# Gates as three bf16 parts in both expert mixtures, weight loads in pieces, and two projection jobs moved, in a 12-stage perceiver kernel

## The reference, cut to what matters

```python
# L1_ffn: one expert of eight, its gate is a sigmoid
logits = x @ gate_w.T; sel = argmax(logits); rw = sigmoid(max(logits))
for e in range(8):
    xs = x * (rw * (sel == e))[:, None]
    out = out + (xs @ w_up[e].T) * silu(xs @ w_gate[e].T) @ w_down[e].T
# L2_ffn: two experts of eight, gates a softmax over both, and two shared experts without a gate
logits = x @ router_w + router_b
gates = softmax(logits where it is among the two largest, else -inf)
out = sum_e gates[:, e] * expert_e(x) + shared_0(x) + shared_1(x)     # expert = silu(x w1) * (x w3) @ w2
# L3_xattn: keys and values of all 8192 context rows
k = context @ k_w.T + k_b;  v = context @ v_w.T + v_b;  16 heads of 16 channels, masked softmax
```

## Time and profile before

| | |
|---|---|
| time, median of three runs | 1553.99 us (1551.33 to 1559.85) |
| profiled execution, its own time | 1555.07 us |
| its span in the profile | 1553.2 us |
| PE busy | 1501.2 us, 97% of the span |
| DVE, ACT, POOL busy | 838.6, 639.3, 151.7 us |
| mean granted clock of PE | 0.994 |

### The profile page before, as it was taken

One profiled execution on the slowest core, in us unless ns is written; L12 is line 12 of the kernel. 1 busy time (PEld: TensorE's weight loads), 2 busy tenths in 40 slices (PEclk: granted clock), 3 DMA queues, 4 the chain that ended last, 5 costly groups with the idle time before them and its releaser, 6 DMA issues.

```text
span 1553.2 us, 24376 instructions
## 1 busy us (share of the span) xinstructions
PE 1501.2 (97%) x9939; PEld 960.1 (62%) x9950; DVE 838.6 (54%) x1488; ACT 639.3 (41%) x1213; POOL 151.7 (10%) x191
## 2 busy tenths in 40 slices
PE   8999999999999999999999999999999999998898
PEld 3667656886668655567655544555555554645697
DVE  5652645643432533432362258889899983566422
ACT  1212342122432423433353246777777775404121
POOL 0000340002000212200102051100000000100000
PEclk9999999999999999999999999999999999999999
DMA  9134132221023420112215166464567404100140
GB/s 373 58 108 175 69 119 89 82 82 62 0 83 114 154 69 28 38 58 104 81 42 177 65 157 123 80 93 69 122 140 180 67 4 182 65 34 1 48 170 14
DMA packets 40406, 146.87 MB, mean 95 GB/s; under 512 B 6092, under 2 KB 21708, under 8 KB 30668
## 3 DMA queue, kind: packets, MB, share of 16 engines
q1 hardware_dynamic: 40296, 145.32, 32.5%
HBM read 122.73 MB, written 22.56 MB: 94 GB/s over the span
## 4 chain that ended last, share of the span: by engine, by line
PE 87%; DVE 8%; ACT 3%; issue 1%; DMA 0%; SPq 0%; ACTq 0%; DVEq 0%
PE PS L162 54%; PE PS L2107 8%; PE PS L2019 7%; PE PS L2004 5%; PE PS L612 3%; PE PS L1434 2%; DVE SM L2123 1%; PE PS L1628 1%; PE PS L1446 1%; PE PS L2636 1%; PE PS L1641 1%; DVE CN L2687 1%; PE PS L2098 1%; PE PS L1648 1%; PE PS L2569 1%
## 5 line engine op out<-in xcount | busy, mean ns | idle before, releaser
L2123 DVE TENSOR_REDUCE SM<-PS 128x1 f32<-128x1024 f32 x256 | 301.7, 1219 | 35.4 <-PE PS L2004 34.2
L162 PE MATMUL PS<-CT,HT 128*128 128x512 f32 x416 | 190.4, 593 | 0.7 <-ACT HT L719 0.7
L162 PE MATMUL PS<-CN,AR 128*128 128x256 f32 (+1 forms) x832 | 188.0, 371 | 0.0
L162 PEld LDWEIGHTS PS<-CN,AR 128*128 128x128 f32 x832 | 151.0, 190 | 44.0 <-issue 28.7
L2019 PE MATMUL PS<-AR 49*128 49x256 bf16 (+1 forms) x1216 | 163.5, 272 | 3.0 <-issue 2.4
L162 PE MATMUL PS<-HT,AR 128*128 128x512 f32 x328 | 149.5, 605 | 2.6 <-ACT HT L346 1.6
L2019 PE MATMUL PS<-AR,CT 49*128 49x256 bf16 (+1 forms) x832 | 125.2, 272 | 0.0
L669 DVE TENSOR_REDUCE SM<-AR 128x1 f32<-128x512 f32 x96 | 65.7, 686 | 97.2 <-ACT AR L725 95.6
L162 PEld LDWEIGHTS PS<-CT,HT 128*128 128x128 f32 x416 | 73.6, 190 | 68.4 <-issue 66.0
L162 PEld LDWEIGHTS PS<-HT,AR 128*128 128x128 f32 x328 | 60.7, 191 | 86.1 <-issue 82.0
L162 PE MATMUL PS<-AR 128*128 128x256 f32 (+3 forms) x504 | 109.8, 372 | 1.4 <-DVE AR L647 0.8
(11 more groups left out here) (340 smaller groups left out, 2142.5 us busy)
## 6 DMA issues: line engine op xcount, KB each, us to landing
CN<-ctx_n SPq DMA_DIRECT2D x24, 1024.0 KB, 4.7
AR<-k_parts SPq DMA_DIRECT2D x114, 128.0 KB
CT<-pack SPq DMA_DIRECT2D x7, 2048.0 KB, 8.4
k_parts<-CN SPq DMA_DIRECT2D x32, 384.0 KB, 3.3
AR<-pack SPq DMA_DIRECT2D x20, 512.0 KB, 4.8
CT<-k_parts SPq DMA_DIRECT2D x78, 128.0 KB
CN<-v_ones SPq DMA_DIRECT2D x8, 1152.0 KB, 10.3
v_ones<-CN SPq DMA_DIRECT2D x29, 288.0 KB, 2.9
```

Of the source, the lines that this page charges most:

```text
L162: last = te.matmul(o, l, r, start=first and k == 0, stop=final and k == n - 1, skip_group_check=True)
L2123: ve.tensor_reduce(MX9[:, p % 2, e, g % 8 // 4, g % 4:g % 4 + 1], PS[:, b:b + 2, :].rearrange("p a b -> p (a b)"), AX, ALU.max).then_inc(* ...
```

## The change

It does these things, in the diff's order:

1. `esel` becomes bf16 (half the bytes), with ones for every row r whose r mod 8 is e, 48 rows in all; a bf16 identity `idb` is loaded too.
2. The gates are split into three bf16 parts whose sum is the fp32 gate. R has 24 columns in stage 5 and 48 in stage 8 (three parts for each of two choices). The four transposes and the per-expert product are bf16: one matmul with K = 24 or 48, in place of one fp32 matmul with K = 8.
3. The routing chains on DVE change: in stage 5 four small instructions for the parts, threaded through the chain, and a wider last product. In stage 8 the second choice's push is one instruction, only the second logit's exponential is taken, the weights are 1/(1+ex) and ex/(1+ex), four instructions split them, and two products make R.
4. `up` is cut in `gate` and `up`. Stage 5: `gate(0)`, the transposes, half job 0, `up(0)`. Stage 8: `gate(0)`, `up(0)`, the `r8` job, the transposes, `gate(1)`.
5. Stage 8's half jobs `h8` go. That value job is dealt to `s9` in place of a key job, and this key job to `heads`, at g = 33.
6. Stage 10's weights come in eight transfers of up to 512 KB at g = 81, 83, ... 95, each behind the scores of the step before. The fetches that stood at the first step of pair 8 (g = 64) stand at g = 67, behind a score of that pair.

```diff
-    "s5": [("gate", 16), ("esel", 1024)] + ...
+    "s5": [("gate", 16), ("esel", 512), ("idb", 64)] + ...
-                             ("s7", "v"), ("b8", "kvkv"), ("t8", "k"), ("r8", "v"), ("h8", "v"), ("b9", "vvk"),
-                             ("t9", "k"), ("s9", "kvvkvvvkvv"), ("heads", "k" * 4)):
+                             ("s7", "v"), ("b8", "kvkv"), ("t8", "k"), ("r8", "v"), ("b9", "vvk"),
+                             ("t9", "k"), ("s9", "kvvkvvvvvv"), ("heads", "k" * 5)):
...
+        def gate_rows_pe(pe, s, R, idb):
+            b, before = PB.take(("rt", s), ("rt", s))
+            pe.wait_ge(*before, ("R", s))
+            for i in range(4):
+                z = pe.e.transpose(PS[:, b, 0:256].bitcast(BF16)[0:R.shape[2], tok(i)], R[:, i, :], idb)
+            z.then_inc(*pe.inc("turned", "rt_ps", s))
...
-                up(0)
-                jobs_pe(pe, f"r{s}")
-                rows8_pe(pe, s, R)
-                half_pe(pe, f"h{s}", 0)
+                gate(0)
+                if gate_first:
+                    gate_rows_pe(pe, s, R, idb)
+                    half_pe(pe, f"h{s}", 0)
+                    up(0)
+                else:
+                    up(0)
+                    jobs_pe(pe, f"r{s}")
+                    gate_rows_pe(pe, s, R, idb)
+                    gate(1)
                 for e in range(n):
...
-                        te.matmul(PS[:, b, :], W["esel"][0:8, e * 128:e * 128 + 128], RT, start=True, stop=True,
+                        te.matmul(PS[:, b, :], esel[0:RT.shape[0], e * 128:e * 128 + 128], RT, start=True, stop=True,
...
                     if e + 1 < n:
+                        if e or gate_first:
+                            gate(e + 1)
                         up(e + 1)
                     if e:
                         down(e - 1)
-                half_pe(pe, f"h{s}", 1)
+                if gate_first:
+                    half_pe(pe, f"h{s}", 1)
                 down(n - 1)
...
+            ve.tensor_copy(parts5[:, :, 0], rw5).then_inc(*dv.inc("route", "rw_p0", 5))
...
+            ve.tensor_tensor(rest5, rw5, parts5[:, :, 0], ALU.subtract).then_inc(*dv.inc("route", "rw_rest", 5))
+            ve.tensor_tensor(parts5[:, :, 1], rw5, parts5[:, :, 0], ALU.subtract).then_inc(*dv.inc("route", "rw_p1", 5))
...
+            ve.tensor_tensor(parts5[:, :, 2], rest5, parts5[:, :, 1], ALU.subtract).then_inc(
+                *dv.inc("route", "rw_p2", 5))
+            dv.wait_ge(("oh", 5), ("rw_p2", 5))
+            ve.tensor_tensor(R5.rearrange("p a (k e) -> p a k e", k=3),
+                             oh5.unsqueeze(2).to_broadcast([128, 4, 3, 8]),
+                             parts5.unsqueeze(3).to_broadcast([128, 4, 3, 8]), ALU.mult).then_inc(
+                *dv.inc("route", "R", 5))
...
-        for p in range(4):
+        for p in range(5):
             PAIR_JOBS[8 * p + 1] = jobs.pop(0)
...
+        W10_PIECES = [(to[:, c:min(c + 1024, to.shape[1])], src[:, c:min(c + 1024, to.shape[1])])
+                      for to, src in (w10_load, w10_more) for c in range(0, to.shape[1], 1024)]
+        W10_AT = {81 + 2 * i: piece for i, piece in enumerate(W10_PIECES)}
...
-                if what in ("beside", "both") and n % 8 == k == 0:
+                if what in ("beside", "both") and n % 8 == (3 if n // 8 == 8 else 0) and k == 0:
...
+                    if p == 8:
+                        used.append(("st_ps", 9, 8, 4, 1))
...
-                if what == "beside" and (n, k) == (80, 0):
-                    sp.wait_ge(("job_ps", "k", 31), ("job_ps", "v", 31))
-                    for load in (w10_load, w10_more):
-                        se.dma_start(*load).then_inc(*sp.lands("w10", "w", 10))
+                if what == "beside" and k == 0 and n in W10_AT:
+                    sp.wait_ge(("job_ps", "k", 31), ("job_ps", "v", 31), ("st_ps", 9, n // 8, 2 * (n % 8) - 1, 1))
+                    se.dma_start(*W10_AT[n]).then_inc(*sp.lands("w10", "w", 10))
```

More of the change, by code:

```diff
@@ L32 @@
     "s4": [("Wq", 512), ("Wk", 512), ("Wv", 512), ("gamma", 1)],
-    "s5": [("gate", 16), ("esel", 1024)] + [(f"{k}{e}", 256) for e in range(8) for k in ("g", "u", "d")],
+    "s5": [("gate", 16), ("esel", 512), ("idb", 64)] + [(f"{k}{e}", 256) for e in range(8) for k in ("g", "u", "d")],
     "s6": [("Wq", 512), ("Wk", 512), ("Wv", 512), ("bq", 2), ("bk", 2), ("bv", 256)],
@@ L36 @@
            ("dsel", 128), ("rows", 4)],
-    "s8": [("rw", 16), ("rb", 32), ("esel", 1024)] + [(f"{k}{e}", 256) for e in range(10) for k in ("g", "u", "d")],
+    "s8": [("rw", 16), ("rb", 32), ("esel", 512), ("idb", 64)] + [(f"{k}{e}", 256) for e in range(10) for k in ("g", "u", "d")],
     "s9": [("Wq", 512), ("Wk", 512), ("Wv", 512), ("bq", 2), ("bk", 2), ("bv", 256), ("sum34", 34),
@@ L1414, in experts, with gate @@
             ready = lambda e: ("h", s, "gated" if gate_first else "row" if e < n_gated else "up", e)
+            esel, idb = W["esel"].bitcast(BF16), W["idb"].bitcast(BF16)
             def pe_part(pe):
                 te = pe.e
-                def up(e):
-                    wg, wu = mat(W[f"g{e}"], 2), mat(W[f"u{e}"], 2)
+                def gate(e):
+                    wg = mat(W[f"g{e}"], 2)
                     b, before = PB.take(("g", s, e), ("g", s, e))
@@ L1849, in dve_8 @@
             dv.wait_ge(("oh", 8))
-            ve.tensor_scalar(l8, oh8, -3e38, None, ALU.mult).then_inc(*dv.inc("route", "out", 8))
-            dv.wait_ge(("out", 8))
-            ve.tensor_tensor(l8, l8, lg8, ALU.add).then_inc(*dv.inc("route", "lg2", 8))
-            first_of_max_dve(dv, 8, "oh2", l8, top8b, eq8b, m8b, oh8b, ("lg2", 8))
-            dv.wait_ge(("oh2", 8))
-            ve.tensor_tensor(oh8b, oh8b, oh8, ALU.add).then_inc(*dv.inc("route", "both", 8))
-            ve.tensor_tensor(ex8, lg8, up8(top8), ALU.subtract).then_inc(*dv.inc("route", "under", 8))
@@ L1857, in dve_8 @@
[L1857 to L1864 removed]
+            ve.scalar_tensor_tensor(out=l8, in0=oh8, scalar=-3e38, in1=lg8, op0=ALU.mult, op1=ALU.add).then_inc(
+                *dv.inc("route", "lg2", 8))
@@ new lines, in dve_8 @@
+            dv.wait_ge(("lg2", 8))
+            ve.tensor_reduce(top8b, l8, AX, ALU.max).then_inc(*dv.inc("route", "oh2_top", 8))
+            dv.wait_ge(("oh2_top", 8))
+            ve.tensor_tensor(ex8, top8b, top8, ALU.subtract).then_inc(*dv.inc("route", "under", 8))
+            ve.tensor_tensor(eq8b, l8, up8(top8b), ALU.is_equal).then_inc(*dv.inc("route", "oh2_eq", 8))
+            dv.wait_ge(("oh2_eq", 8))
+            ve.tensor_tensor(eq8b, eq8b, CS["iota8"].rearrange("p (a b) -> p a b", b=8), ALU.mult).then_inc(
+                *dv.inc("route", "oh2_w", 8))
@@ new lines, in dve_8 @@
+            dv.wait_ge(("w_rest", 8), ("w_p1", 8))
+            ve.tensor_tensor(parts8[:, :, 2, :], rest8, parts8[:, :, 1, :], ALU.subtract).then_inc(
+                *dv.inc("route", "w_p2", 8))
+            dv.wait_ge(("w_p2", 8), ("oh2", 8))
+            for n, oh in enumerate((oh8, oh8b)):
+                ve.tensor_tensor(R8[:, :, 24 * n:24 * n + 24].rearrange("p a (k e) -> p a k e", k=3),
+                                 oh.unsqueeze(2).to_broadcast([128, 4, 3, 8]),
+                                 parts8[:, n].rearrange("p k a -> p a k").unsqueeze(3).to_broadcast([128, 4, 3, 8]),
+                                 ALU.mult).then_inc(*dv.inc("route", "R", 8))
@@ L3026, in _constants @@
     c["ones2"] = (np.arange(128)[:, None] % 64 == 32).astype(np.float32)
-    esel = np.zeros((128, 8, 128), np.float32)
-    for e in range(8):
-        esel[e, e, :] = 1.0
-    c["esel"] = esel.reshape(128, 1024)
+    esel = np.zeros((128, 8, 128), np.uint16)
+    for r in range(48):
+        esel[r, r % 8, :] = 0x3F80
+    c["esel"] = esel.reshape(128, 1024).view(np.float32)
+    c["idb"] = (np.eye(128) * 0x3F80).astype(np.uint16).view(np.float32)
     inv = (1.0 / np.float32(10000.0) ** (np.arange(0, 64, 2, dtype=np.float32) / np.float32(64))).astype(np.float32)
```

68 lines of the change are left out of this document (50 added, 18 removed).

## The result

The changed kernel takes 1543.75 us (median of 19 executions, 1538.3 to 1551.3) where the kernel before took 1553.99 us on the same chip (19 executions, 1549.0 to 1559.9). The ratio is 0.9934, its 95% interval 0.9919 to 0.9948: 10.2 us faster. The forecast was 1544.3 us, the range 1538.5 to 1551.5. The total is right. Three terms of the sum are not (the slot of a gate's product, the start of stage 5, and stage 9 beside its large transfers), and a part of the agreement is luck.

The account below looks back on a forecast made before the run. The prediction took PE to bound the kernel, busy 1501.2 of 1553.2 us. Stage 5 -4.8, stage 8 -6.65 and the key job +1.83 gave -9.6, so 1544.3 us from the median 1553.99; range 1538.5 to 1551.5.

Parts of the forecast that it names:

- The slot of a gated expert: Stages 5 and 8, PE time for the gate's product: 0.53 us in place of 1.16, 0.63 less in each of sixteen.
- The 0.1 that was to come back at a bank: Stage 5: 0.1 us regained because expert 1's second product no longer waits for a bank.
- K and the passes: The gate's bf16 product: K = 24 is not slower by its rows than K = 8; K = 49 streams at 0.213 us.
- The start of stage 5: Longer DVE chain to R delays the transposes and the first gate's product: 0.35 us lost, bounds 0 to 1.2.
- Stage 8: Eight slots -5.0, half jobs gone -0.95 and -0.9, +0.2 back: -6.65 us, with R 2 us ahead.
- The key job: Stage 9, key job added at g = 33: +1.83 us, eight steps taking 23.66 us in place of 21.83.
- The transfers: Stage 10's weights in eight transfers in place of two: 0, since the window around the two took 21.84 us.
- The prediction's own sign of being wrong: PE gaps named "issue" at the weight pieces, or PE waiting for RT or a bank in the mixtures.
- The fetches of pair 8: Stage 9, moved from g = 64 to 67: counted 0, ends -3 and +3; PE's 1.72 us gap precedes them.
- The second rival: Stage 9: the gap beside the value loads goes, up to 2.7 us more won, time 1541.6; chance 0.15.
- the slower one: Stage 9 rival: each weight piece brings a gap of 1.7 to 2.9 us, time 1558.2 or 1567.6; chance 0.05.
- The first rival: Stage 5: the new 0.43 us wait drops PE's clock, costing 1.7; with low-bound slots, time 1548.2; chance 0.27.

Follow-up runs that it names:

- Experiment 4: The changed kernel with the gate's product in fp32 again, everything else as changed: 1555.23 us, against 1543.75 for the changed kernel.
- the transfers alone: The kernel before with only stage 10's weights in eight pieces and pair 8's fetches at g = 67: 1553.37 us, ratio 0.9999.
- experiment 2: Block lateness counted from traces, zero being the whole loop's promptest block; then key fetches issued three at a time: before 1550.34 us, changed 1537.10.
- the jobs alone: The kernel before with only stage 8's half jobs removed, their value job dealt to `s9` and a key job at g = 33: 1558.85 us, ratio 1.0031.
- spread fetches: Stage 9's key fetches issued three at a time instead of six: before 1550.34 us, before with jobs moved 1551.52, changed 1537.10 (second set 1542.88).

## Why the prediction was right or wrong

**The slot of a gated expert** was mis-sized: 0.53 was forecast, 0.43 measured, the low bound of the slot. The change back from bf16 to fp32 costs nothing that shows: 0.10 us behind the product, as between any two groups. The 0.10 read from the earlier trace rows came from two bf16 products between jobs with other readers and weights; the slots here show that it is not the change of type, and what it was there is open. Sixteen slots at 0.73 are -11.7 in place of -10.1. The 0.1 that was to come back at a bank did not: from expert 1's first `up` product to its gate's product it is 3.63 us in both kernels.

**K and the passes.** No run has a bf16 product with K = 8, but with K = 24 and with K = 48 the slot is the same 0.43, and in fp32 K = 24 costs the same 1.16 as K = 8. Experiment 4 shows that the product's type is what paid: the whole gain of the gates goes with it.

**The start of stage 5** cost 0.09, not 0.35. The order of events was the one forecast; R and with it the transposes came 0.17 us earlier (1.78 behind the logits' copy, not 1.95), and from there to the first gate's product it was 3.11, not 3.20. DVE's copy of RT took 0.41 in place of 0.68 and ended 2.3 us before its reader.

**Stage 8**: -7.49 for -6.65, at the same clock; the difference is the slot again (8 x 0.10). R was ahead by 2.7 us where 2 were forecast.

**The key job**: +1.82 for +1.83. **The transfers**: 0 as a median (ratio 0.9999), but not for the reason given. I read from one window of 21.84 that loads in this stretch bring no gap. A window without a gap was a matter of which block fell due when. The prediction's own sign of being wrong, a gap named "issue" at the pieces, did come, and so did its counterpart: the windows there were not 21.84 but 22.85 and 22.50. The total hid it, since more had gone elsewhere.

**The fetches of pair 8 and the gap of the earlier trace rows.** "The gap stands before the moved fetches are issued" was true and beside the point: the block it waited for went out 2.5 us before the gap's end, behind the value loads and the earlier keys. The prediction also read the gap into a window that starts behind it. Most of it lies in the window ahead, which is 1.0 us over 21.84:

```profile
1097.28:1120.12 22.84, 20.92 (x282) 11.43 (x278) 20.45 (x25) 16.87 (x33) 0.00 (x0) 1.00 0.74 165
```

Of the 3.8 in the next window 1.3 are the statistics (23.10 without a late block), about 1.7 the low clock (mean 0.93 over 25.62 us), and the gap's remaining 0.7 or so. The second rival, that the gap goes, came true (-4.2 in the four windows from 1052.88 to 1145.74) together with a piece of the slower one (+1.7 beside the pieces), and neither was in the sum. Each is read from one execution, and with the transfers alone the gap at step 62 changed by 0.8 us with nothing ahead of it changed, so a part of both is scatter. Between the profiled executions the difference was -13.2 for -9.6: -1.8 in the mixtures, -2.6 net in stage 9, -0.6 in the rest, +1.4 by the clock at the start. Between the medians it was -10.2. That the forecast lies 0.6 us from the median is partly this scatter, and not earned to the last digit.

**The clock in stage 5** did not fall, though the new wait was there (0.25 us of standing): in none of the nine profiles with the new start. The first rival did not come. The Trainium skill ("TensorE: Matmul & The Clock Gate", section "HAM oscillation — how this bites in real kernels") tells of idle stretches between bursts of products that bring the low clock back; its case is a wait for transfers at every tile, which neither place here is. In stage 8, with a wait of 0.33 us ahead of the same tiny products, the clock was low in seven of twelve profiles (5.38 us), and in stage 5, with one of 0.25 us a product group behind them, in none of nine. So a short wait alone does not decide it, and what does stays open.

## What to carry to other kernels

Where one small fp32 product stands alone in a stream of fp32 products, its type sets its price: three bf16 parts stacked along K in one bf16 product took 0.43 us in place of 1.16, sixteen times over. Before a gap called "issue" is laid to an engine, look at the instruction queue: a long, straight program needs its next block in time, and a burst of data transfers can hold it up. Where a transfer is not needed soon, a few at a time are then better than all of them early. Count PE's recorded instructions up to each gap: if the gaps stand at one place of a round of 256, they are block borders. And an idle product should write a bank outside the ring, or it deals everybody behind it another one.

## What the runs showed of the hardware

- Instruction blocks wait behind data. By the zero of the whole loop (experiment 2), the eight blocks behind gaps of 1.6 to 2.4 us were fetched 8.8 to 9.8 us late, and a block less than 7.4 us late brought no gap of over 0.4 us. All 21 gaps of over 0.4 us named "issue" in stage 9's loop stand at the border of a block (instruction 191 to 193 of a round of 256 recorded ones) and end 2.4 to 3.2 us after a packet's start. At six of the eight gaps of over 1.5 us the granted clock fell to 1.2 GHz within 2 us of the gap's end; at the changed kernel's and at the 1.72 us one of the jobs alone it did not.
- The same kernel scatters by 8 to 13 us between executions where such blocks are near the edge (before in its sets of 15 and more; changed: 1538.3 to 1551.3 in 19), and with spread fetches by 2.5 to 5.7, though in sets of 5 to 11. Fewer executions show less scatter by themselves: nine of the kernel before lay within 4.5 us.
- A single bf16 product between fp32 products pays nothing that shows for the change of type: 0.12 us ahead of it and 0.10 behind, as between fp32 groups.
- DVE copies a 24 x 512 bf16 tile out of PSUM in 0.41 us, and the 8 x 512 fp32 tile took 0.68.
- 128 satisfied waits in a row took PE 3.6 us, 28 ns each.
